# Mask stage of a graph network kernel: weighing the key one-hots on DVE in place of POOL

## What is computed

```
h = relu(layernorm(x));  x0 = h
for each of two layers:
    h1 = relu(x[row] @ nbW + nbb);  h2 = relu(x[col] @ selfW + selfb)
    gate = sigmoid(log(u) - log1p(-u) + concat(h1, h2) @ attW + attb)
    mask = clip(gate * (ZETA - GAMMA) + GAMMA, 0, 1)
    rowsum = segment_sum(mask, row) + EPS_DEG
    d = clip(rowsum ** -0.5, 0, 10)
    x_next = segment_sum((mask * d[row] * d[col]) * x[col], row)
out = x + x0 + x1 + x2
```

## Time and profile before

| | |
|---|---|
| median of 3 runs | 6730.72 us (6729.32 to 6736.85) |
| the profiled execution's own time | 6725.77 us |
| its span | 6723.7 us |
| busy in the span | PE 4115.6, DVE 5556.7, ACT 2500.0, POOL 2252.7 us |
| mask stage, layer 0 | about 1850 to 2690 us |
| mask stage, layer 1 | about 4370 to 5210 us |

### The profile page before, as it was taken

The page is one execution under the profiler, slowest core; times in us unless marked ns, Lnnn a source line. Parts: engine busy times, 40 slices in busy tenths (PEclk is TensorE's granted clock), DMA queues, the critical chain, the costliest instruction groups (busy, mean ns, idle before and its releaser), DMA issues. The chain is left out here.

```text
span 6723.7 us, 166891 instructions
## 1 busy us (share of the span) xinstructions
PE 4115.6 (61%) x58388; PEld 3656.1 (54%) x58388; DVE 5556.7 (83%) x10207; ACT 2500.0 (37%) x5126; POOL 2252.7 (34%) x1874
## 2 busy tenths in 40 slices
PE   3777777765855555355557777855555255557666
PEld 2666666654545554344556676555554245446666
DVE  8999999995399999899966665099999899976666
ACT  2656566642344443355510001344443255520000
POOL 0000000000089998000025453089998000024444
PEclk9777777765555555677778888555555576768888
DMA  2000000002365654799979986165554799989888
GB/s 64 0 0 0 0 0 0 0 1 15 69 204 194 197 196 150 240 332 333 332 241 246 244 245 179 41 198 199 197 196 146 239 331 332 332 249 246 240 247 230
DMA packets 438059, 1160.67 MB, mean 173 GB/s; under 512 B 211241, under 2 KB 216974, under 8 KB 437402
## 3 DMA queue, kind: packets, MB, share of 16 engines
q1 hardware_dynamic: 316671, 549.99, 26.5%
q0 software_dynamic: 75264, 354.33, 19.5%
q10 hardware_dynamic: 46036, 255.30, 10.0%
HBM read 936.26 MB, written 281.94 MB: 181 GB/s over the span
## 5 line engine op out<-in xcount | busy, mean ns | idle before, releaser
L582 POOL DMA_INDIRECT work<-msg_d,widx x444 | 552.5, 1244 | 2075.1 <-issue 1620.4
L1577 PE MATMUL psG<-y_window,area 128*128 128x64 bf16 x14976 | 686.1, 219 | 764.4 <-DVE area L1225 595.9
L1577 PEld LDWEIGHTS psG<-y_window,area 128*128 128x128 bf16 x14976 | 642.2, 116 | 808.6 <-issue 501.5
L1590 PE MATMUL psG<-work,edge 112*128 112x192 bf16 x7104 | 794.3, 282 | 393.3 <-DVE edge L1260 392.8
L1590 PEld LDWEIGHTS psG<-work,edge 112*128 112x128 bf16 x7104 | 750.9, 151 | 436.3 <-DVE edge L1260 357.1
L638 ACT ACTIVATE work<-iota,work 128x149 bf16<-128x149 f32 x2496 | 788.9, 406 | 0.0
L1399 PE MATMUL psG<-area,work 128*128 128x112 bf16 x2496 | 551.0, 390 | 339.1 <-DVE area L967 339.1
L1399 PEld LDWEIGHTS psG<-area,work 128*128 128x128 bf16 x2496 | 357.6, 148 | 487.5 <-issue 344.0
L1392 PE MATMUL psG<-work,merge 128*128 128x148 bf16 x4992 | 542.8, 293 | 69.8 <-ACT work L638 69.8
L1392 PEld LDWEIGHTS psG<-work,merge 128*128 128x128 bf16 x4992 | 526.1, 131 | 92.3 <-issue 66.2
L745 ACT ACTIVATE edge<-merge,npid 128x2048 bf16<-128x2048 uint16 x156 | 312.4, 2003 | 705.3 <-DMA merge<-crel_d 705.3
(11 more groups left out here) (254 smaller groups left out, 8162.5 us busy)
## 6 DMA issues: line engine op xcount, KB each, us to landing
msg_d<-work ACTq DMA_DIRECT2D x312, 784.0 KB, 4.7
area<-rlo_d SPq DMA_DIRECT2D x312, 512.0 KB, 4.4
merge<-crel_d SPq DMA_DIRECT2D x312, 512.0 KB, 5.4
area<-crelp_d SPq DMA_DIRECT2D x312, 512.0 KB, 5.8
y_window<-y_d SPq DMA_DIRECT2D x312, 48.0 KB, 3.7
work<-msg_d,widx POOLq DMA_INDIRECT x444
y_d<-cur SPq DMA_DIRECT2D x7, 1008.0 KB, 3.8
y_d<-work SPq DMA_DIRECT2D x7, 1008.0 KB, 4.8
```

Source lines behind the costliest of these rows:

```text
L582: pool.indirect_dma_start(out=windows[par][0:WP, g, :, :].rearrange("p s w -> p (s w)"), out_offset=None, in_=msg_d, in_offset=bass.Indire ...
L1577: ins = pe.matmul(psG[:, 2 * h + k // CH, k % CH * D:(k % CH + 1) * D], col_one_hots[:, h, k * P:(k + 1) * P], y_window[:, h, m * D:(m + 1 ...
L1590: ins = pe.matmul(psG[:, slot_, 0:MW], q_one_hots[slot_][0:WP, g, :, s], windows[slot_][0:WP, g, s, 0:MW], start=g == 0 and s == 0, stop=g ...
```

## The change

DVE does the two multiplications of a pair that POOL did. They stand in a new function `weigh_rows`, which DVE calls for pair p_ - 1 at the head of the step of pair p_, right behind `h_hots(p_)` in its order, and once more at the end for the last pair; the first step is taken out of the loop. DVE waits there for a new semaphore `mask_split`, which POOL raises when the three parts are made. POOL keeps the minimum, the copy and the split. The parts are now laid out part by part and double buffered (`m v e` in place of `e m`), and POOL waits for `weighted_ready` before it overwrites them. `h_hots` no longer waits for `weighted_ready`, since both are DVE's. Neither `h_hot` nor `weighted` changes its layout, and PE's instructions stay the same.

```diff
--- before.py
+++ after.py
@@ -199,10 +199,10 @@
         q_bc = bcast[:, :, :].rearrange("p a e -> p (a e)").rearrange("p (u e) -> p u e", u=2)
         h_hot = scratch[:, 0:2 * HW * CT].bitcast(bf16).rearrange("p (v u n j) -> p v u n j", v=2, u=2, j=CT)
         weighted = [t.rearrange("p (u j m n) -> p u j m n", u=2, j=CT, m=3) for t in (scratch[:, 800:800 + 3 * HW * CT].bitcast(bf16), far[:, 12000:12000 + 6 * HW * CT])]
-        mask_parts = scratch[:, 1960:1960 + 3 * CT].bitcast(bf16).rearrange("p (e m) -> p e m", m=3)
-        mask_rest = scratch[:, 2020:2020 + 2 * CT]
-        mask_now = scratch[:, 2130:2130 + 2 * CT]
-        gate = scratch[:, 2060:2060 + 4 * CT].rearrange("p (v e) -> p v e", v=2)
+        mask_parts = scratch[:, 1952:1952 + 6 * CT].bitcast(bf16).rearrange("p (m v e) -> p m v e", m=3, v=2)
+        mask_rest = scratch[:, 2050:2050 + 2 * CT]
+        mask_now = scratch[:, 2150:2150 + 2 * CT]
+        gate = scratch[:, 2084:2084 + 4 * CT].rearrange("p (v e) -> p v e", v=2)
         q_hot = [t[:, 4 * ST // 2:8 * ST // 2].bitcast(bf16).rearrange("p (v u e) -> p v u e", v=2, u=2) for t in (cur, work)]
         lo_hot = [t[:, 0:4 * ST // 2].bitcast(bf16).rearrange("p (v u n k) -> p v u n k", v=2, u=2, k=CT) for t in (cur, work)]
         junk = [t.rearrange("p (k n) -> p k n", k=CH) for t in (flat_merge[:, 0:CH * HI], scratch[:, 0:CH * HI])]
@@ -264,7 +264,7 @@
         y_ready, y_stored = sem("y_ready"), sem("y_stored")
         weighted_by_act, weighted_by_dve = sem("weighted_by_act"), sem("weighted_by_dve")
         dist_ready, logits_ready, sigmoid_ready, general_step = (sem(n) for n in ("dist_ready", "logits_ready", "sigmoid_ready", "general_step"))
-        odd_hot_ready, extras_ready, gate_ready, parts_step, weighted_ready, row_sums_kept = (sem(n) for n in ("odd_hot_ready", "extras_ready", "gate_ready", "parts_step", "weighted_ready", "row_sums_kept"))
+        odd_hot_ready, extras_ready, gate_ready, parts_step, weighted_ready, row_sums_kept, mask_split = (sem(n) for n in ("odd_hot_ready", "extras_ready", "gate_ready", "parts_step", "weighted_ready", "row_sums_kept", "mask_split"))
         mask_turn, mask_turn_kept, mask_stored, mask_loaded, row_lane_loaded, lane_columns_stored = (sem(n) for n in ("mask_turn", "mask_turn_kept", "mask_stored", "mask_loaded", "row_lane_loaded", "lane_columns_stored"))
         span_ready, widest_ready, local_ready, b_ready, b_stored = (sem(n) for n in ("span_ready", "widest_ready", "local_ready", "b_ready", "b_stored"))
         lo_loaded, crel_loaded, msg_index_loaded, y_window_loaded = ([sem(f"{n}{h}") for h in range(2)] for n in ("lo_loaded", "crel_loaded", "msg_index_loaded", "y_window_loaded"))
@@ -547,7 +547,7 @@
                     for v in range(2):
                         p_ = i * 2 + v
                         cols = bass.ds(p_ * 2 * CT, 2 * CT)
-                        done = (L * TP + p_) * 5
+                        done = (L * TP + p_) * 4
 
                         def step(n, ins):
                             ins.then_inc(parts_step, 1)
@@ -557,15 +557,13 @@
                         pool.nop(nofuse=True)
                         step(1, pool.tensor_scalar(mask_now[:, :], gate[:, v, :], 1.0, None, ALU.min))
                         pool.tensor_copy(ga[:, cols], mask_now[:, :]).then_inc(mask_ready, 1)
-                        step(2, pool.tensor_copy(mask_parts[:, :, 0], mask_now[:, :]))
-                        step(3, pool.tensor_tensor(mask_rest, mask_now[:, :], mask_parts[:, :, 0], ALU.subtract))
-                        step(4, pool.tensor_copy(mask_parts[:, :, 1], mask_rest))
-                        step(5, pool.tensor_tensor(mask_parts[:, :, 2], mask_rest, mask_parts[:, :, 1], ALU.subtract))
-                        for u in range(2):
-                            wait(pool, sums_added, L * T + p_ * 2 + u - 3)
-                            pool.nop(nofuse=True)
-                            pool.tensor_tensor(weighted[v][:, u, :, :, :], h_hot[:, v, u, :, :].rearrange("p n j -> p j n").unsqueeze(2).to_broadcast([P, CT, 3, HW]),
-                                               mask_parts[:, u * CT:(u + 1) * CT, :].unsqueeze(3).to_broadcast([P, CT, 3, HW]), ALU.mult).then_inc(weighted_ready, 1)
+                        wait(pool, weighted_ready, L * T + p_ * 2 - 2)
+                        pool.nop(nofuse=True)
+                        step(2, pool.tensor_copy(mask_parts[:, 0, v, :], mask_now[:, :]))
+                        step(3, pool.tensor_tensor(mask_rest, mask_now[:, :], mask_parts[:, 0, v, :], ALU.subtract))
+                        step(4, pool.tensor_copy(mask_parts[:, 1, v, :], mask_rest))
+                        pool.tensor_tensor(mask_parts[:, 2, v, :], mask_rest, mask_parts[:, 1, v, :], ALU.subtract).then_inc(mask_split, 1)
+
                 with pool.If(is_local):
                     steps(pool, 0, T // 4, split_masks)
                 with pool.Else():
@@ -1120,7 +1118,6 @@
                     dve.tensor_scalar(col_hot[:, v, 0, :], crel_bc[:, 0, :], pid[:, 0:1], None, ALU.is_equal).then_inc(one_hot_ready[1], 1)
 
                 def h_hots(p_, v):
-                    wait(dve, weighted_ready, L * T + p_ * 2 - 2)
                     dve.tensor_tensor(h_hot[:, v, :, :, :], hwin[:, :, :].unsqueeze(1).to_broadcast([P, 2, HW, CT]),
                                       hb[:, bass.ds(p_ * 2 * CT, 2 * CT)].rearrange("p (u j) -> p u j", u=2).unsqueeze(2).to_broadcast([P, 2, HW, CT]), ALU.is_equal).then_inc(hi_one_hot_ready, 1)
 
@@ -1141,9 +1138,18 @@
                         dve.tensor_tensor(lo_hot[L][:, v, u, :, :], iota16[:, :, :],
                                           lof[:, bass.ds(t * CT, CT)].unsqueeze(1).to_broadcast([P, P, CT]), ALU.is_equal).then_inc(lo_one_hot_ready, 1)
 
+                def weigh_rows(p_, v):
+                    dve.wait_ge(mask_split, L * TP + p_ + 1)
+                    for u in range(2):
+                        wait(dve, sums_added, L * T + p_ * 2 + u - 3)
+                        dve.tensor_tensor(weighted[v][:, u, :, :, :], h_hot[:, v, u, :, :].rearrange("p n j -> p j n").unsqueeze(2).to_broadcast([P, CT, 3, HW]),
+                                          mask_parts[:, :, v, u * CT:(u + 1) * CT].rearrange("p m j -> p j m").unsqueeze(3).to_broadcast([P, CT, 3, HW]), ALU.mult).then_inc(weighted_ready, 1)
+
                 def local_masks(i):
                     for v in range(2):
                         p_ = i * 2 + v
+                        if not isinstance(i, int) or p_ > 0:
+                            weigh_rows(p_ - 1, 1 - v)
                         if not isinstance(i, int) or p_ + 2 < TP:
                             hots(p_ + 2, v)
                         choose(p_, v)
@@ -1180,7 +1186,9 @@
                     for v in range(2):
                         hots(v, v)
                     h_hots(0, 0)
-                    steps(dve, 0, T // 4, local_masks)
+                    local_masks(0)
+                    steps(dve, 1, T // 4, local_masks)
+                    weigh_rows(TP - 1, 1)
                     dve.wait_ge(row_sums_ready, L + 1)
                     dve.tensor_reduce(abr[:, 0, :], psR[:, 1, 0:3 * HI].rearrange("p (m h) -> p h m", m=3), AX.X, ALU.add).then_inc(row_sums_kept, 1)
                 with dve.Else():
```

## The result

| | median (runs) | median of before | ratio, 95% interval | pair period, layer 0 |
|---|---|---|---|---|
| before | 6730.0 us (4) | | | 10.60 us |
| **after** | **7091.5 us** (4, 7074.9 to 7098.0) | 6730.0 | **1.0535** (1.0512 to 1.0559) | 13.01 us |

The change made the kernel slower by 5.35%. Of the kernel after, the profiled execution took 7097.95 us; its span is 7096.2, 372.5 us more than before. The pair period is the distance between the first and the last addition of products (L1135 before, L1132 after) in layer 0, over 77.

The account below looks back on a forecast made before the run. DVE was taken to set the pace of the mask stages. -3.27 + 4.37 + 1.3 = +2.40 us a pair over 2 x 76 intervals (+365 us), plus 4 for the ends, gave 7100 us, range 6930 to 7195.

Parts of the forecast that it names:

- (a): Per pair on DVE: without POOL's two multiplications, each L1141 falls from 2.851 to 1.216 us, -3.27 us.
- (b): Per pair on DVE: two added multiplications of 1152 elements at 2.26 us each, +4.37 us after overlap.
- (c): Per pair on DVE: waiting for `mask_split` from POOL's small steps, +1.3 us; ends 0.2 and 1.9.
- (d): Terms at nothing: POOL's wait for `weighted_ready`, `h_hots` without its wait, the layout of the parts; PE's work unchanged.
- The ends: Each layer: first interval grows about 8 us, tail shrinks from 15.1 to 9.5; together +2 us, +4 for both.
- The split in time: Rival on DVE's wait: split ready in time, wait 0.2 us, +1.30 a pair, 6933 us; chance 0.10.
- a weighing at one element a step: Rival on DVE's multiplications: one element a step, wait stays, +0.57 us a pair, 6822 us; chance 0.10.
- the two together: Rival on DVE: multiplications of 1.35 us and no wait, -0.73 us a pair, 6624 us, faster; chance 0.06.
- Weighing at POOL's rate: Rival on DVE's multiplications: 3.18 us each as on POOL, +4.24 us a pair, 7379 us; chance 0.06.

Follow-up runs that it names:

- pool_memset: Kernel before, with each of POOL's two multiplications of a pair replaced by a memset of the same output, so POOL reads nothing there; 6364.8 us, one run.
- read_straight: Changed kernel whose weighing alone reads `h_hot` in the order in which it lies, giving other row sums; 6802.2 us, one run.
- layout_jn: Changed kernel with `h_hot` and `hwin` laid out key column innermost, so both readers read `h_hot` in a row; 6771.0 us, ratio 1.0068 to before.
- weigh_late: Changed kernel with the weighing of pair p - 1 moved behind the three one-hots on DVE; 6935.7 us, ratio 1.0314 to before.
- copy_last: Changed kernel with POOL's copy of the mask moved behind the split, one step less in the chain; 7022.8 us, ratio 1.0448 to before.
- shared_jn: Changed kernel with `h_hot` key column innermost, DVE's weighing behind `choose`, and POOL doing one of a pair's two multiplications; 6446.1 us, ratio 0.9582 to before.

## Why the prediction was right

7100 us were forecast and 7091.5 measured, in the range of 6930 to 7195. The mechanism came true term by term. For the profiled execution the sum was +369 us against 372.5, and that closeness is in part luck: the two stages gave 360, and 12 came from parts that the change does not touch. By the prediction's own count, from pair 1 on, the period of layer 0 went from 10.64 to 12.97 us, +2.33 where +2.40 was forecast.

- **(a) L1141.** -3.27 us a pair forecast, 2 x (2.851 - 1.222) = -3.26 measured. The reason holds by pool_memset.
- **(b) The weighing.** 2.26 us each forecast from L1130, 2.26 measured; +4.37 for the two, and from the start of one pair's weighing to the next instruction in the timeline it is about 4.35. That L1130's rate came from its read of `h_hot` was an inference then; read_straight shows it. The ground on which half the rate was ruled out, L946's repeated element, was shown once more by layout_jn's L1121, 0.558 to 0.958 us when its operand came to repeat.
- **(c) The wait.** 1.3 us forecast; 1.32 measured in the mean of all pairs, 1.28 without the first of a layer. The steps were near, not exact: L559 ended 0.07 us after L1138, and the step that stood behind L1121 was held up by 0.33. weigh_late and copy_last show that the wait is this chain: it shrank when DVE's work was put ahead of it and when a step was taken out.
- **(d) The ends and the terms at nothing.** The first interval grew by 8.7 us in layer 0 and 6.4 in layer 1, for a forecast of 8, and the tail shrank by 5.7, as forecast (15.1 to 9.5). 16 matmuls of PE took 1.20 us as before. L1127 fell by 0.04 us, which I hadn't counted, and the gap behind it from 0.08 to 0.03 in the mean; the two together are as large as the 0.07 us by which the period came out shorter than forecast.
- **The rivals.** The split in time (6933 us), a weighing at one element a step (6822) and the two together (6624) did not come true; the second has its counterpart in read_straight, 6802 us, where the read was in a row in fact. Weighing at POOL's rate (7379) did not come true either: for the same access DVE took 2.26 us and POOL at least 2.69.

What was wrong came later, in the expectations: a floor for the period of 9.8 us, read from loads and ACT steps in a kernel with a period of 10.6. pool_memset had a period of 8.47.

## What to carry to other kernels

Before work is moved to the engine that sets the pace, price it by a row of that engine with the same access pattern, and count the chain that has to be over before it can start. Here the freed 3.26 us were real, but a hopping read made each moved multiplication cost 2.26 us in place of 1.36, and its place in the order exposed a chain of small steps that DVE's own neighbouring instructions held up. Where two engines keep each other waiting for reads of SBUF, as POOL and DVE do here, put the long instruction of one beside those of the other that did not wait, as in shared_jn. And a least period is only seen in a kernel that reaches it.

## What the runs showed of the hardware that was not expected

- A small POOL instruction that reads SBUF ends 0.07 to 0.15 us after the DVE instruction that it stood behind, and DVE's next one isn't longer for it: L1138 was 1.222 us in the mean and L1121 0.558 with such steps in between, in the kernel after. In the timelines above the small steps get one turn for each DVE instruction; what they cost DVE is the wait for the last of them.
- For the same 1152 elements, a read with hops of 32 bytes cost DVE 2.26 us against 1.355, and POOL 2.69 against 2.12.
- In the kernel with POOL's memsets, DVE's two-source L1140 ran at its full speed beside them, and so did they (1.06 us). The single-source one-hots L1117 and L1119 did not: all 37 memsets that took longer, up to 1.60 us, ran beside one of them, and L1119 took up to 1.63 us in place of 0.75.
